# A two-layer graph network: the keys that layer 1 broadcasts, as 8-bit integers

## The reference, cut to what matters

```python
x = _layernorm(x + _L0_gnn_ref(x, src, dst, edge_attr_64, ...))
# layer 1
msg = x[src] * edge_weight[:, None]
agg = jax.ops.segment_sum(msg, dst, num_segments=x.shape[0])
h = jax.nn.relu((agg + x) @ W1 + b1)
x = _layernorm(x + h @ W2 + b2)
```

## Time and profile before

| | |
|---|---|
| time, median of 3 runs | 3341.38 us (3341.27 to 3345.3) |
| span of the profiled execution, first to last instruction | 3345.5 us |
| nearest run to it | 3345.3 us |
| VectorE busy | 2535.8 us (76%) |
| GpSimd busy | 2373.9 us (71%) |
| TensorE busy (matmul) | 1942.4 us (58%) |
| ScalarE busy | 983.0 us (29%) |
| mean DMA rate | 180 GB/s |
| `source_rows`: first key load issued, and GpSimd's first activity of the next stage | 2574.56 and 2994.67 us |

### The profile page before, as it was taken

How to read it: one execution, slowest core, us unless ns; L and a number is a source line. 1 busy time by engine, 2 the same in 40 slices (tenths; PEclk the granted TensorE clock), 3 DMA queues, 4 the chain that set the end, 5 groups by cost and what they waited for, 6 DMA issues and landing times. The chain is left out here.

```text
span 3345.5 us, 49252 instructions
## 1 busy us (share of the span) xinstructions
PE 1942.4 (58%) x14474; PEld 1231.9 (37%) x14474; DVE 2535.8 (76%) x4772; ACT 983.0 (29%) x2092; POOL 2373.9 (71%) x2260
## 2 busy tenths in 40 slices
PE   2565555555555555555555555535674666657886
PEld 2222222222222222222222222215663655547776
DVE  6577777777777777777777777747996999988987
ACT  3222222222222222222222222213565666640001
POOL 0477777777777777777777777773454888868876
PEclk7788788888888877878788888768897677769999
DMA  9733333233333333333333333318895999989997
GB/s 302 188 108 94 94 94 94 94 94 94 94 94 94 97 98 94 95 100 94 94 94 94 94 94 94 94 47 313 293 334 186 357 357 358 357 323 401 405 396 296
DMA packets 219438, 601.78 MB, mean 180 GB/s; under 512 B 96208, under 2 KB 113488, under 8 KB 206648
## 3 DMA queue, kind: packets, MB, share of 16 engines
q1 hardware_dynamic: 139498, 376.13, 34.3%
q0 software_dynamic: 67488, 210.15, 17.0%
q10 hardware_dynamic: 12309, 13.63, 1.5%
HBM read 403.92 MB, written 195.84 MB: 179 GB/s over the span
## 5 line engine op out<-in xcount | busy, mean ns | idle before, releaser
L1123 POOL DMA_INDIRECT region_rows<-x_space,pos x1664 | 1633.2, 982 | 547.6 <-issue 504.9
L980 PE MATMUL ps_cnt<-ident,work 128*128 128x128 f32 x832 | 180.5, 357 | 799.6 <-DVE work L1064 799.6
L907 ACT CAST x_space<-ps_cnt 128x512 bf16<-128x512 f32 x208 | 122.0, 586 | 1460.6 <-PE ps_cnt L980 1460.6
L980 PEld LDWEIGHTS ps_cnt<-ident,work 128*128 128x128 f32 x832 | 118.6, 179 | 974.5 <-issue 974.5
L973 PE MATMUL ps_fx<-work,w_wf 128*128 128x512 f32 x416 | 265.9, 724 | 137.2 <-ACT work L897 135.3
L1053 DVE TENSOR_REDUCE rank<-work 128x8 f32<-128x784 f32 x208 | 323.2, 1554 | 21.4
L1033 DVE COPY x_space<-edges_space 128x16 f32 (+1 forms) x208 | 38.5, 185 | 335.2 <-DMA region_rows<-x_space,pos 335.2
L1069 DVE TENSOR_TENSOR ps_agg<-ps_cnt,x_space 128x512 f32<-128x512 f32 x208 | 145.6, 700 | 131.4 <-ACT x_space L907 131.4
L966 PE MATMUL ps_fx<-work,x_space 128*64 128x512 bf16 x1248 | 241.2, 507 | 0.0
L943 PE MATMUL ps_th<-x_space,w_wf 128*128 128x512 f32 x416 | 224.9, 624 | 16.2 <-DMA x_space<-rbf 16.2
L1049 DVE TENSOR_TENSOR work<-onehot,ps_rank 128x784 f32<-128x784 bf16 x208 | 202.0, 971 | 7.1
(11 more groups left out here) (256 smaller groups left out, 5132.6 us busy)
## 6 DMA issues: line engine op xcount, KB each, us to landing
tmp_space<-region_rows SPq DMA_DIRECT2D x98, 882.0 KB, 6.5
tmp_space<-key_rows SPq DMA_DIRECT2D x98, 576.0 KB, 6.9
x_space<-rbf SPq DMA_DIRECT2D x104, 512.0 KB, 3.7
tmp_space<-rel_rows SPq DMA_DIRECT2D x104, 512.0 KB, 4.0
run_rows<-x_space SPq DMA_DIRECT2D x60, 873.0 KB, 5.5
run_rows<-work SPq DMA_DIRECT2D x38, 873.0 KB, 5.7
region_rows<-x_space,pos POOLq DMA_INDIRECT x1664, 2.3
x_space<-part_rows SPq DMA_DIRECT2D x208, 48.0 KB, 2.6
```

What stands on the lines that cost most here:

```text
L980: last = e.transpose(ps_cnt[:, t * P:(t + 1) * P], product[:, t * P:(t + 1) * P], ident[:, :])
L1123: e.indirect_dma_start(out=region_rows, out_offset=bass.IndirectOffsetOnAxis(ap=pos[j][:, t:t + 1], axis=0), in_=rows_f[j][:, t, :], in_of ...
```

## The change

The DRAM array of keys, the buffer `across` and the five broadcast buffers become unsigned 8-bit integers. ScalarE's copy from PSUM converts to 8 bits; the DMAs carry half the bytes; VectorE's compare reads 8-bit keys and writes bf16 as before. The buffers behind `key_bc` in `tmp_space` begin at a lower address.

```diff
--- before.py
+++ after.py
@@ -6,6 +6,7 @@
 F32 = mybir.dt.float32
 BF16 = mybir.dt.bfloat16
 I32 = mybir.dt.int32
+U8 = mybir.dt.uint8
 ALU = mybir.AluOpType
 ACT = mybir.ActivationFunctionType
 AX = mybir.AxisListType
@@ -1139,7 +1140,7 @@
         upper_parts = spaces[1][:, 0:NB * D].bitcast(BF16).rearrange("p (b c d) -> p b c d", c=2, d=D)
         low_parts = spare[:, 0:NB * D // 2].bitcast(BF16).rearrange("p (b d) -> p b d", d=D)
         x1_part = lambda b, c: low_parts[:, b, :] if c == 2 else upper_parts[:, b, c, :]
-        across = spare[:, NB * D // 2:NB * D // 2 + KW // 2].bitcast(BF16).rearrange("p (c q) -> p c q", q=P)
+        across = spare[:, NB * D // 2:NB * D // 2 + KW // 4].bitcast(U8).rearrange("p (c q) -> p c q", q=P)
         by_part = lambda ps: ps[:, 0:PARTS * D].rearrange("p (c d) -> p d c", c=PARTS)
 
         def center(e, step, at):
@@ -1547,8 +1548,8 @@
             own = stage_sems(0)
             KB, OB, FLAT = 5, 5, 3
             U = CAPT // 2
-            key_bc = [tmp_space[:, u * (CAP // 2):(u + 1) * (CAP // 2)].bitcast(BF16) for u in range(KB)]
-            at = KB * CAP // 2
+            key_bc = [tmp_space[:, u * (CAP // 4):(u + 1) * (CAP // 4)].bitcast(U8) for u in range(KB)]
+            at = KB * CAP // 4
             which = [tmp_space[:, at + u * (U * P // 2):at + (u + 1) * (U * P // 2)].bitcast(BF16) for u in range(2)]
             at += U * P
             msg = [tmp_space[:, at + u * U * D:at + (u + 1) * U * D].rearrange("p (t d) -> p t d", d=D) for u in range(2)]
@@ -2331,7 +2332,7 @@
     rel_rows = nc.dram_tensor("rel_rows", (NG * T, P), BF16).ap()
     region_rows = nc.dram_tensor("region_rows", (NB * STRIDE + P * T, RW // 2), F32).ap()
     run_rows = nc.dram_tensor("run_rows", (NB * CAP + TAIL, SW), BF16).ap()
-    key_rows = nc.dram_tensor("key_rows", (-(-NB * CAPT // P) * P, P), BF16).ap()
+    key_rows = nc.dram_tensor("key_rows", (-(-NB * CAPT // P) * P, P), mybir.dt.uint8).ap()
     program(nc, n_nodes, n_edges, ap["x"], ap["x_t"], ap["src"], ap["dst"], ap["dst_next"], ap["dst_rows"], ap["firsts"],
             ap["group_dst"], ap["ew"], ap["rbf"],
             {k: ap[f"w_{k}_dram"] for k in w}, out, wxh_rows, x1_rows, sorted_rows, q_block_row, seed_rows, rel_rows,
```

## The result

The changed kernel takes 3470.76 us (median of 4 runs, 3466.51 to 3472.07), the kernel before 3341.96 us beside it: 1.0386 times as long, 95% interval 1.0374 to 1.0398, +129 us. The forecast was 3471 us. The profiled execution has a span of 3468.3 us and a time of 3469.96.

The account below looks back on a forecast made before the run. Taken as bound: VectorE and GpSimd excluding one another, 2.09 us a half block. Altered turns, +1.35 us a block over 97 blocks, give +131, less 1 for the first load: 3341.4 + 130 = 3471 us, range 3390 to 3585.

Parts of the forecast that it names:

- The compare's price: VectorE's 196 compares: 8-bit keys lose the fourfold rate but keep the doubled one, +0.30 us each.
- The turns: VectorE and GpSimd exclude one another; who asks first goes first, so order alternates: +1.35 us a block, +131 us.
- The size: A block in the compare's stage takes 5.52 us in place of 4.17; over 97 blocks +131, in all +130 us.
- The first load: VectorE's only wait for keys, at the stage's start: halved bytes save 3 us at most, 1 taken.
- Writing the keys: Transposed keys written in 128-byte pieces in place of 256, ahead of the stage: slack, so nothing.
- ScalarE's copies: Two copies to `across` ahead of the key write, same element count: nothing.
- unchanged within 2 us: Claim for the profile after: all stages other than the compare's keep their time within 2 us.
- Strict turns (B): L1615 wins over waiting GpSimd, order stays, each half grows by 0.30 alone: +59 us, 3400 us; chance 0.23.
- GpSimd always first (C): GpSimd's subtraction gets its turn before L1615 in every half, 3.32 us a half: +240, 3581 us; chance 0.14.
- No difference (D): The compare keeps the fourfold rate and only the first load is shorter: 3340 us; chance 0.05.
- The transfers as the bound (E): DMA transfers set the stage's pace at 358 GB/s, so halved key loads free it: -60, 3281 us; chance 0.03.

Follow-up runs that it names:

- run 6: Changed kernel (8-bit keys) with GpSimd's subtraction cut to one of its nine tiles: 3340.83 us against 3347.18 for the kernel before, ratio 0.998.
- run 7: Kernel before (bf16 keys, full loads) with GpSimd's subtraction cut to one of its nine tiles: 3301.26 us against 3347.18, ratio 0.9867.
- run 3: Changed kernel plus a wait holding GpSimd's subtraction until the compare two halves on has ended: 3988.73 us against 3930.62 for the kernel before.
- Run 9: Kernel before (bf16 keys) with VectorE's compare moved behind the third part, no other work: 3419.96 us against 3351.14, ratio 1.0208.
- run 1: Kernel before with bf16 keys but only half of each block's keys loaded: 3932.66 us against 3930.62, ratio 1.000.
- run 5: Kernel before with a bf16 compare doing twice the elements (2304): 3472.67 us against 3347.18, ratio 1.0376.
- run 2: Kernel before with only the compare reading 8-bit, all 576 KB still loaded: 4061.4 us against 3930.62, ratio 1.0328.
- run 8: Kernel before (bf16 keys) with GpSimd's subtraction cut to one of nine tiles and half the key bytes loaded: 3279.6 us against 3347.18.

## Why the prediction was right

**The compare's price.** +0.30 us, from the pair L1024 and L534, was 0.29 to 0.30 (runs 6 and 7, and the stage's start). The 8-bit operand takes the fourfold rate away and leaves the doubled one. Section 5.1 of Vector Engine (DVE) Microarchitecture Reference in the Trainium skill asks 2-byte operands for the fourfold mode and no type for the doubled one over both read ports; the 8-bit rows agree with it (0.80 us against 0.51 for 1152 elements).

**The turns.** Who asks first gets the way, also between two VectorE instructions that follow each other. GpSimd's lead in the second half was put at 0.19 us and is 0.17; it was enough in every block of the steady state. Of the 131 us worked out, the part that is stream (58) and the part that is order (73) could be separated, by run 3. Run 9 moves the order with no other cost and lands within 3 us of the same arithmetic (+69 for +71).

**The size.** 5.52 us a block were forecast, 5.50 came in the mean: the product's successor starts after 0.66 to 0.67 us and the compare's after 0.73, not 0.74. The stage grew by 127.3 us for 130. The forecast is off by 0.2 us only, and that is luck: runs of one kernel are 4 to 6 us apart.

**The small terms.** The first load: VectorE's idle time before the first compare fell from 10.9 to 10.2 us, 0.7 for the 1 that was taken. Writing the keys, ScalarE's copies and the other stages moved nothing that stands out of the runs' scatter. But "unchanged within 2 us" was too narrow for the other stages: the two profiles differ by 6.9 us ahead of the stage and by 2.4 behind it.

**The rivals.** Strict turns (B) is what the kernel does when the wait of run 3 forces it, at the +58 us for the +59 that B was given. GpSimd always first (C) didn't come: a lead of 0.13 us is enough for L1616. No difference (D) falls with the compare's rate. The transfers as the bound (E) falls with run 1. The Trainium skill, SBUF — State Buffer, section 'A bandwidth-pool intuition that's wrong', gives about 358 GB/s between HBM and a core; run 7 moved 401 for 300 us, and the measurement decides.

No version here beats the kernel before with the whole work done. Run 7 shows what doing a ninth of GpSimd's subtraction gives, 46 us with the transfers as they are; the work would have to go elsewhere, and that wasn't tried. That the clock of TensorE fell without a cost follows from run 3 and 5 (same clock, different times) and from VectorE never waiting for TensorE in steady state; nothing varied the clock by itself.

## What to carry to other kernels

Where two engines exclude one another, an engine that is busy for 100% of a stage may be standing: set its instructions' durations against the same instruction unhindered, and look whose end they stick to. Smaller elements weren't cheaper to compare: an 8-bit operand halved VectorE's rate (0.80 us for 1152 elements instead of 0.51), and if that makes an instruction outlast the moment at which the other engine asks, the order of turns flips and can cost more than the instruction itself. A wait that holds the other engine back for 0.4 us (GpSimd starts 1.93 us after the product in run 3, and asked after 1.53) can then be worth nearly 2% (73 of 4061 us here).

## What was not expected of the hardware

TensorE's granted clock in the stage went from a mix (0.72) to 1.2 GHz throughout (0.50) in the changed kernel and in runs 2, 3 and 5, where halves follow one another every 2.39 to 2.75 us instead of 2.09. It was 0.87 and 1.00 (all at 2.4 GHz) in runs 7 and 8, with a half every 1.86 and 1.76 us. A longer stand of TensorE between halves doesn't explain it: by the windows' busy times it stands 0.77 us a half in run 3 (clock 0.50), 0.74 in the kernel before and 0.80 in run 8 (clock 1.00). The cause stays open. One chip took some 580 us more for what lies ahead of `source_rows`, nearly all of it `sorted_messages`, in all of its kernels alike, with this stage unchanged; why isn't known.
